# Expert pairs in a Trainium2 transformer layer: each engine does the oldest pair first, with the lags between the steps unchanged

## The reference

```python
logits = jnp.einsum('bld,ed->ble', x, gate_w)
top_w, top_idx = jax.lax.top_k(logits, TOP_K)          # TOP_K = 2
top_w = jax.nn.softmax(top_w, axis=-1)
dispatch = jnp.zeros((T, E), xf.dtype).at[jnp.arange(T)[:, None], idx].add(wk)
h = jax.nn.silu(jnp.einsum('td,ehd->teh', xf, w1))     # 256 -> 128 for each expert
moe = jnp.einsum('teh,te,edh->td', h, dispatch, w2)    # 128 -> 256
return moe.reshape(B, L, D) + shared
```

## Time and profile before

| what | us |
|---|---|
| median of 3 runs (lowest, highest) | 903.46 (901.47, 910.64) |
| span of the profiled execution, first to last instruction | 941.9 |
| expert pairs in the profiled execution, first transpose to last scatter | 719.0 to 870.8 |
| shared block and last norms in it, after the last O | 864.4 to 941.9 |

### The profile page before, as it was taken

One profiled execution on the slowest core, in us unless ns is written; L12 is line 12 of the kernel. 1 busy time (PEld: TensorE's weight loads), 2 busy tenths in 40 slices (PEclk: granted clock), 3 DMA queues, 4 the chain that ended last, 5 costly groups with the idle time before them and its releaser, 6 DMA issues. The chain is left out here.

```text
span 941.9 us, 14973 instructions
## 1 busy us (share of the span) xinstructions
PE 789.9 (84%) x4690; PEld 491.1 (52%) x4690; DVE 652.5 (69%) x1256; ACT 519.9 (55%) x1047; POOL 370.8 (39%) x442
## 2 busy tenths in 40 slices
PE   4688998999989989899688779899978877778884
PEld 3433343443434434334233358777757777777773
DVE  4488689797887988967679457777644444443785
ACT  1226577776777767767567633344324554545363
POOL 4430171631715417144100104566650555556342
PEclk9869799998999999989989989999999888988997
DMA  7856528737578275672664013453545344445994
GB/s 153 236 119 179 123 62 203 158 105 168 91 179 177 92 178 96 151 175 88 151 113 181 1 48 108 141 179 120 169 157 176 113 143 131 134 140 184 268 180 90
DMA packets 112421, 133.29 MB, mean 142 GB/s; under 512 B 16724, under 2 KB 80726, under 8 KB 112344
## 3 DMA queue, kind: packets, MB, share of 16 engines
q1 hardware_dynamic: 98616, 108.39, 45.9%
q0 software_dynamic: 13248, 23.15, 9.4%
q10 hardware_dynamic: 480, 0.79, 0.5%
HBM read 68.18 MB, written 59.87 MB: 136 GB/s over the span
## 5 line engine op out<-in xcount | busy, mean ns | idle before, releaser
L480 DVE TENSOR_REDUCE negmax<-ring 128x2 f32<-128x1024 f32 x256 | 307.0, 1212 | 85.1 <-PE ring L643 84.0
L430 ACT ACTIVATE probs<-scores 128x512 f32<-128x512 f32 x498 | 273.6, 599 | 110.8 <-PE scores L661 107.7
L661 PE MATMUL scores<-q_st,k_st 64*128 64x512 f32 x498 | 207.5, 475 | 30.2 <-ACT probs L430 15.1
L643 PE MATMUL ring<-k_st,q_st 48*128 48x512 f32 x512 | 185.6, 480 | 22.5 <-DMA k_st<-rows_in 7.2
L661 PEld LDWEIGHTS scores<-q_st,k_st 64*128 64x128 f32 x498 | 83.7, 192 | 178.3 <-ACT probs L430 108.4
L675 PE MATMUL av<-probs,v_aug 128*32 128x512 f32 x1024 | 142.5, 630 | 6.3 <-ACT probs L430 6.3
L331 POOL CAST part_r<-negmax 128x16 fp32r<-128x16 f32 x32 | 7.6, 237 | 210.0 <-DVE negmax L480 210.0
L643 PEld LDWEIGHTS ring<-k_st,q_st 48*128 48x128 f32 x512 | 72.6, 198 | 33.3 <-issue 20.4
L1534 POOL DMA_INDIRECT rows_out<-m_y,projected x48 | 47.3, 985 | 66.0 <-ACT m_y L1599 53.2
L166 POOL TENSOR_TENSOR scratch<-qk_raw,cos 128x512 f32<-128x512 f32 x29 | 37.1, 1278 | 79.5 <-ACT qk_raw L383 78.4
L1685 DVE TENSOR_TENSOR m_h_lo<-scores,m_h_hi 128x512 fp32r<-128x512 f32 x40 | 27.7, 692 | 53.7 <-ACT m_h_hi L1585 42.9
(11 more groups left out here) (253 smaller groups left out, 1672.2 us busy)
## 6 DMA issues: line engine op xcount, KB each, us to landing
q_st<-rows_in SPq DMA_DIRECT2D x96, 128.0 KB, 4.6
k_st<-rows_in SPq DMA_DIRECT2D x90, 128.0 KB, 5.5
experts<-split SPq DMA_DIRECT2D x8, 1024.0 KB
projected<-records SPq DMA_DIRECT2D x48, 129.0 KB
split<-O SPq DMA_DIRECT2D x24, 256.0 KB, 2.8
experts<-rows_out SPq DMA_DIRECT2D x10, 512.0 KB, 9.8
m_rows<-records SPq DMA_DIRECT2D x32, 129.0 KB, 2.1
X<-in_x SPq DMA_DIRECT2D x8, 512.0 KB, 5.0
```

Source lines behind the costliest of these rows:

```text
L430: nc.scalar.activation(probs[r // 2 % 2][r % 2][:, a, :], score_of(R)[:, a, :], ACT.Exp, scale=HD ** -0.5).then_inc(exp_done, 1)
L480: nc.vector.tensor_reduce(negmax[Gn % 2][:, t, 2 * p:2 * p + 2], ring[t % 2][:, :, :], AX.X, ALU.max, negate=True).then_inc(max_done, 1)
L643: last = nc.tensor.matmul(half[:, a, :], q[rows, t * P:(t + 1) * P], k[rows, :], start=True, stop=True)
L661: nc.tensor.matmul(score_of(R)[:, a, :], k[rows, kt * P:(kt + 1) * P], q[rows, :], start=True, stop=True).then_inc(sc_ps, 1)
```

## The change

Each of the three engines does the work of a step from the oldest pair to the newest: on PE O(s-3), T(s-2), H(s), X(s+1); on ACT Y(s-3), GH(s-2), SI(s-1), XH(s+1); on DVE GL(s-2), R(s), XL(s+1). All lags stay, but that of Y, which comes one step earlier (s-3 and no longer s-4), so that the loop has one step less. No instruction is added or removed. SP's and POOL's loops are unchanged. The diff:

```diff
-        STEPS = range(-X_AHEAD, PAIRS + OUT_LAG + 1)
+        STEPS = range(-X_AHEAD, PAIRS + OUT_LAG)
@@ scalar
-                x, i, t, o = s + X_AHEAD, s - SILU_LAG, s - TURN_LAG, s - OUT_LAG - 1
-                if of(x):
-                    act.wait_ge(xt_s, x + 1)
-                    if x > 1:
-                        act.wait_ge(mh_s, x - 1)
-                    nc.scalar.copy(x_hi[x % 2], bank_x[x % 2]).then_inc(xhi_s, 1)
+                x, i, t, o = s + X_AHEAD, s - SILU_LAG, s - TURN_LAG, s - OUT_LAG
+                if of(o):
+                    act.wait_ge(my_s, o + 1)
+                    if o >= HELD:
+                        act.wait_ge(sent[(o - HELD) % LOADS], 32 * ((o - HELD) // LOADS + 1))
+                    for f in range(2):
+                        nc.scalar.activation(y[o % HELD][:, f, :], bank_o[o % 2][:, f, :], ACT.Copy,
+                                             scale=rows[o % LOADS][:, f, D:D + 1]).then_inc(scaled_s, 1)
                 if of(t):
...
                 if of(i):
                     act.wait_ge(pre_s, i + 1)
                     nc.scalar.activation(g[i % 2][:, :, :], g[i % 2][:, :, :], ACT.Silu).then_inc(msilu_s, 1)
-                if of(o):
...
+                if of(x):
+                    act.wait_ge(xt_s, x + 1)
+                    if x > 1:
+                        act.wait_ge(mh_s, x - 1)
+                    nc.scalar.copy(x_hi[x % 2], bank_x[x % 2]).then_inc(xhi_s, 1)
@@ vector
-                if of(x):
-                    dve.wait_ge(xhi_s, x + 1)
-                    nc.vector.tensor_tensor(x_lo[x % 2], bank_x[x % 2], x_hi[x % 2].bitcast(F32), ALU.subtract).then_inc(xlo_s, 1)
                 if of(t):
...
+                if of(x):
+                    dve.wait_ge(xhi_s, x + 1)
+                    nc.vector.tensor_tensor(x_lo[x % 2], bank_x[x % 2], x_hi[x % 2].bitcast(F32), ALU.subtract).then_inc(xlo_s, 1)
@@ tensor
-                if of(x):
-                    pe.wait_ge(loaded[x % LOADS], 32 * (x // LOADS + 1))
-                    if x > 1:
-                        pe.wait_ge(xlo_s, x - 1)
+                if of(o):
+                    pe.wait_ge(glo_s, o + 1)
+                    if o > 1:
+                        pe.wait_ge(scaled_s, 2 * (o - 1))
...
+                if of(x):
+                    pe.wait_ge(loaded[x % LOADS], 32 * (x // LOADS + 1))
+                    if x > 1:
+                        pe.wait_ge(xlo_s, x - 1)
                     for f in range(2):
                         for c in range(DC):
-                            last = nc.tensor.transpose(bank_x[x % 2][:, f, c, :], rows[x % LOADS][:, f, c * P:(c + 1) * P], ident[:, :])
-                    last.then_inc(xt_s, 1)
...
+                            last = nc.tensor.transpose(bank_x[x % 2][:, f, c, :], rows[x % LOADS][:, f, c * P:(c + 1) * P], ident[:, :])
+                    last.then_inc(xt_s, 1)
                 if s == PAIRS:
                     transposes(EARLY)
-                if of(o):
-                    pe.wait_ge(glo_s, o + 1)
...
```

More of the change, by code:

```diff
@@ L1757, in tensor @@
                     pe.load(at_r[n:n + AT], tables_i[0:1, 2 * s:2 * s + AT])
-                if of(x):
-                    pe.wait_ge(loaded[x % LOADS], 32 * (x // LOADS + 1))
-                    if x > 1:
-                        pe.wait_ge(xlo_s, x - 1)
+                if of(o):
+                    pe.wait_ge(glo_s, o + 1)
+                    if o > 1:
+                        pe.wait_ge(scaled_s, 2 * (o - 1))
                     for f in range(2):
-                        for c in range(DC):
-                            last = nc.tensor.transpose(bank_x[x % 2][:, f, c, :], rows[x % LOADS][:, f, c * P:(c + 1) * P], ident[:, :])
-                    last.then_inc(xt_s, 1)
+                        at = expert_of(2 * o + f)
+                        for k, (a, w) in enumerate(((g_lo, 0), (g_hi, 1), (g_hi, 0))):
+                            last = nc.tensor.matmul(bank_o[o % 2][:, f, :], a[o % 2][:, f, :], experts[:, bass.ds(at + W2 // P, D // P), w, :],
+                                                    start=f == 0 and k == 0, stop=f == 1 and k == 2, skip_group_check=True)
+                    last.then_inc(my_s, 1)
                 if of(t):
@@ L1784, in tensor @@
                     last.then_inc(mh_s, 1)
+                if of(x):
+                    pe.wait_ge(loaded[x % LOADS], 32 * (x // LOADS + 1))
+                    if x > 1:
+                        pe.wait_ge(xlo_s, x - 1)
+                    for f in range(2):
+                        for c in range(DC):
+                            last = nc.tensor.transpose(bank_x[x % 2][:, f, c, :], rows[x % LOADS][:, f, c * P:(c + 1) * P], ident[:, :])
+                    last.then_inc(xt_s, 1)
                 if s == PAIRS:
                     transposes(EARLY)
-                if of(o):
-                    pe.wait_ge(glo_s, o + 1)
[L1789 to L1796, removed]
             for i in range(EARLY, B):
```

## The result

The new kernel is slower: 919.08 us (median of 4 runs, 917.9 to 921.51) against 906.89 for the kernel before, run beside it; the ratio is 1.0144, 95% interval 1.0107 to 1.0181. The ratios are taken over fast runs alone and so differ a little from the quotients of these medians. By the medians the loss is 12 to 15 us. Forecast were 22, with the loss, its place and the loop behind it as stated, and a size that is too large by 7 to 10.

The account below looks back on a forecast made before the run. The old expert stage was taken to be bound by POOL's scatters, 2.57 us per pair. The 941.9 span less 38.4 of late arrivals, plus 22.4 from the new 3.15 us loop, gave 925.9, stated as 925.5, range 917 to 932.

Parts of the forecast that it names:

- The new loop: Expert stage: H, X, XH, XL and back to H set 3.15 us per pair, PE idling about 0.85.
- ACT and DVE: Expert stage: their work fits inside the 3.15 us step, cost 0; at most 0.3 per pair without the cover.
- The clock: Rival: PE's idling in each expert step lowers its clock, up to 4.3 us per pair; 937 us, chance 0.12.
- the old pace in a timed run: Expert stage before the change: without late arrivals, POOL's scatters bound it at 2.57 us per pair.
- the late arrivals: Expert stage: news of finished matmuls reaches ACT 4 us late every 11 us, taken to belong to the profiled execution.
- 38.4 us: Whole kernel: excess of the 941.9 us profiled span over the 903.46 median, put down to late arrivals.
- 36.6: Expert stage: us by which scatters would end sooner, 834.2 instead of 870.8, if POOL alone bound it.
- the old timed pace is between 2.7 and 3.15: Rival: part of the 38 us lies in other stages; at 3.0 per pair 907 us (903 to 912), chance 0.12.
- The tail: After the last O: first addition waits 15.9 us after it or 7.5 after scatters land; 22.4 us net loss.
- The profile of the new kernel: Its profiled execution would still have holes, at 6.3 matmuls per us against 5.7, and span 935 to 955 us.
- The rule on overlapped halves: Skill rule on XH and XL: half their 1.27 us overlapped gives a 2.5 us loop and no cost; not used.
- The first rival: Late arrivals occur in timed runs too: row buffers set 3.56 us per pair before, 3.15 after; 887 us, chance 0.08.

Follow-up runs that it names:

- e2: New kernel with rows loaded two pairs ahead instead of one (X_AHEAD 2); 905.62 us, ratio 1.0001 to the kernel before.
- e3: New kernel with X moved ahead of H on PE, all else as in the new kernel; 910.29 us, ratio 1.007 to the kernel before.
- e8: New kernel with rows two pairs ahead and GH ahead of Y on ACT; 899.78 us, ratio 0.9942 to the kernel before.
- e1: The kernel before, unchanged, run and profiled a second time; 908.21 us, ratio 1.0023.
- odd execution: The first profiled execution of the kernel before, no edit; span 941.9 us, 3.61 us per pair.
- e9: The new kernel, unchanged, run and profiled again on another occasion; 923.28 us, ratio 1.0162 to the kernel before.
- e6: The kernel before with only Y moved one step earlier (pair s-3, not s-4); 899.47 us, ratio 0.9943.

## Why the prediction was right, and where its size was off

**The new loop** was right in each term: 3.15 us forecast, 3.15 measured; H and X, XH, XL and the hand-over as in pair 0. O and T lie beside XH and XL as said. e2 (rows two ahead) removes the loop and with it the whole loss; e3 (X before H) removes it too, and half of the loss. PE idles 0.57 us per pair by the profile, not 0.85, which counted issue times where the profile counts to the end of the last matmul. ACT and DVE did not lengthen the loop. But ACT's new order isn't free, as I had it: Y ahead of GH makes a loop of its own, 2.77 us in e2 and gone in e8, hidden only because 3.15 is longer.

**The clock**: the rival had 0.12 and didn't happen in the steady part, where the clock was 1.00. It came true for the first four pairs, at 4.42 us per pair where the rival had 4.3, and cost about 4 us: 16.6 for 12.6. The forecast had nothing for it. The holes that it read as "some 3 us" ahead of the low clock were 1.3 to 2.3 us long (759 to 791).

**The step that failed** is the old pace in a timed run. I had reasoned that the late arrivals account for all of the 38.4 us, since 36.6 fitted if POOL's 2.57 bounds. Both halves were wrong. First, the excess was not all in this stage. Against e1, whose span is 43.5 us shorter, the odd execution had 15.6 more before the first X (719.04 for 703.46), 25.5 in the stage (145.4 for 119.9) and 2.4 behind it. The 15.6 are not odd: in the profiles of this record the first X lies anywhere from 703.5 to 721.2 (e2, whose span is 913.1). That 36.6 came near 38.4 was chance. Second, POOL did not bound: the round through nine row buffers takes 9 x 2.84 = 25.6 us, 16.3 of them from X to Y and the other 9.3 for the scatters, their landing (2.68 in the chain of e1) and the next load (3.69). I had added up the round for the new order alone, and found room in it; the sum for the old order, which has a step more between X and Y, was not made. It was the rival "the old timed pace is between 2.7 and 3.15" that came true, at 2.84, and its own rule gives the loss: 40 x (3.15 - 2.84) = 12.4 us. What it lacked was the mechanism: I had it for holes spread thinly over other stages, not for the round.

The sum as it should have been, from e1 and the new kernel: X of pair 0 to pair 10, 25.0 before (703.46 to 728.43) and 35.4 after (706.08 to 741.48), +10.4; pairs 10 to 34, 68.0 and 75.6, +7.6; from there to the last O, 26.9 and 25.4, -1.5; behind it 75.1 and 73.6, -1.5. Together, before rounding, 15.1 us. In e9 the stage is as long as in the new kernel's first profile, 136.4, but what lies behind it took 76.5, so the last term is not clear of the spread. The first term has some 4 us of low clock in it, as said above. Forecast were 13.9 for the second of these terms, 24 x (3.15 - 2.57), which is where 6.3 of the 7.3 us of difference between 22.4 and 15.1 lie. That 15.1 is at the upper end of the 12 to 15 measured is no wonder with one profile of each.

**The tail** was to be 3.6 us shorter. It was 1.5 us shorter than e1's in one profile of the new kernel and 1.4 longer in the other (e9), so no run shows this term.

**The profile of the new kernel** was to have a span of 935 to 955 with holes in it; it had 916.1 and none of that kind, at 192 matmuls in 30 us. e1 had none at 218. So 5.7 matmuls per us is no limit, and recording by itself does not bring the holes: e1 and the new kernel were recorded too, and e1's profiled run, 900.24 us, is the shortest of its 12. No run here shows the rule of the Trainium skill ("NOTIFIC — the notification-queue block", section 7.1) at work, and it lends no support to the conclusion that the late arrivals are not in a typical run, which came out right. What held up PE's semaphores for 4 us every 11 us in that execution stays open: it was seen in one of the 14 profiles here.

**The rule on overlapped halves** ("Perfetto Trace Analysis", "Optimizing Scalar/DVE Operations" in the Trainium skill) speaks of an operation's data-access overhead and not of its whole duration, so the prediction's 2.5 us, with half of 1.27 taken off, was too low even by that rule. It was rightly left out of the sum: in the chain above XH counts 0.60 and XL 0.70, the full durations. In the timeline above XL starts 0.62 us after an XH of 0.59, and H 0.85 after an XL of 0.69: neither dependent started inside the operation that it needs.

**The first rival** (late arrivals in timed runs too, 887) is out by e1 and by the new kernel's time. Its mechanism, the round of row buffers and the step that Y's new place saves, was real: e6 shows it, in the old order.

## What to carry to other kernels

For a software pipeline on engines that work in order, write down for each operation what stands between it and the operation that needs it, on every engine it passes through: "oldest first" with unchanged lags puts the youngest pair's transposes right before the product that needs them, and its round trip over two other engines becomes the period. Where the order is turned round, the lag of what was moved to the end has to grow by one. And add up each ring of buffers for the kernel before as well as for the one after, with the landing times of DMAs in it. When the one profile at hand is longer than every timed run, take the pace neither from it nor from a bound that happens to explain the difference.

## What was not expected of the hardware

Two executions of one program had spans of 941.9 and 898.4 us. In the longer one ACT heard of finished matmuls some 4 us late, in bunches, and the clock had a mean of 0.88 in the stage, against 0.94 in e1. And the time that DMAs take to land is a large part of what bounds this stage in the old order: a load of 129 KB landed between 2.0 and 4.0 us after its issue in e1 (line 1499, min/median/max):

```profile
DMA to landing us min/median/max: 2.0/2.4/4.0
```
